# Two products of a feed-forward block moved into the last head of an attention kernel, the last tile mixed on VectorE, the first stores reordered

## The chip, the cores and the metric

One core of one Trainium2 chip runs the kernel. The metric is the device time of one execution in microseconds (us), the median of several runs. A measurement of this kernel can tell a difference of about 0.2% from none.

## The reference

`X` is 2 x 1024 x 128, all fp32. With `xn = layernorm(X)`:

```python
# differential attention, 16 heads, d = 64
A1, A2 = Q1 @ K1.T / 8, Q2 @ K2.T / 8            # each head: 1024 x 1024
Pm = softmax(A1) - lam * softmax(A2)
Y = concat_heads(Pm @ V) @ Wo + bo
attn = layernorm(Y) * gamma + beta, times 0.2
# feed-forward block: one main set and the best 2 of 8 expert sets per batch row
main = gelu(xn @ W1m + b1m) @ W2m + b2m
expert_out = sum_k gate_k * (gelu(xn @ W1e[k] + b1e[k]) @ W2e[k] + b2e[k])
out = X + attn + a * main + (1 - a) * expert_out
```

## The kernel before, in words

Every engine has its own hand-written stream, and semaphores join them. There are three stages.

**Start.** `X` is loaded, normalised by VectorE (DVE) and transposed by TensorE (PE) into `xT_hi` and `xT_lo` (an fp32 value is split into a high and a low part, and a product takes three passes). Query and key of head 0 are projected (`proj`, L540). Then 32 units `values(u)` (L558) make V for all heads; two units are one tile of 128 tokens. Units below 24 run ahead of the attention (L576), the others in its first steps (`V_LATE`). DVE takes three of four units out of PSUM with the bias added (`evac_v`, L992), ScalarE (ACT) the fourth (`copy_v`, L815), and GpSimd (POOL) adds its bias afterwards (`bias_v`, L498). SyncE (SP) stores each tile in HBM (`store_v`, L319); the SBUF buffer `pt` holds eight tiles, so the evacuation of tile i waits until the store of tile i - 8 has landed. On the same SP queue, in program order: `cross_q` (L285, the halves of q exchanged), `load_w` (L300, the weights of a head), `store_w` (L305, their split parts). On POOL, in order: `split_w(1)` (L405), `start_y` (L419), then `bias_v`.

**Attention.** 32 heads (2 batch rows x 16) of 8 query tiles are 256 steps, `STEPS`; `step(g, k)` with a body of 16 steps stands in each engine's stream (L649 PE, L863 ACT, L508 POOL, L1066 DVE). A step n makes the two score matrices of tile n in PSUM (`product`, L590, L597), takes row maxima on DVE (L1044), exponentials on ACT (`exps`, L830, L838), and POOL mixes them one step later (scale L514, add L517). Three steps later PE transposes the mixed tile in two halves (`turn`, L617), ACT evacuates each half (`evac_pt`, L851, L860), and every four tiles PE multiplies by V (`pv`, L633) and, a step later, by Wo (`out_proj`, L645); DVE adds the result to `y_acc` (`add_y`, L1056). Six PSUM banks are three `slot`s, used in turn by the two score tiles of a step and, at steps 2 and 6 of a head, by a projection for the next head (L550), which ACT and DVE take out. The last head (steps 248 to 255) has no projections. Steps 256 to 262 finish the tiles that are still under way. `beside` puts feed-forward work between them: `start_hidden` (L732) issues products 0 to 3, `start_gelu` (L898) GELUs 0 to 2. `high_w1` (L842, ACT) and `low_w1` (L1061, DVE) split the first-layer weights at the steps in `SPLIT_AT`.

**Feed-forward.** 24 units u (2 batch rows x 3 sets x 4 chunks of the hidden layer). `hidden_mm(u)` (L703, six matmuls, L713) writes a slot; `gelu(u)` (L886, L895) takes it to one of four `hidden` buffers in SBUF; `output_mm(u)` (L718, L726) multiplies that by W2 into banks 6 and 7, where the units of a batch row are summed. The waits that carry the stage are these:

```python
# hidden_mm(u): its slot was that of unit u - 3
after(pe, h_done, u - 2)
# gelu(u): its buffer was that of unit u - 4
act.wait_ge(h_mm, u + 1)
after(act, out_mm, u - 3)
# the order on PE, OUT_LAG = 4
for u in range(OUT_LAG, UNITS + OUT_LAG):
    hidden_mm(u)
    output_mm(u - OUT_LAG)
```

`h_done` counts finished GELUs, `out_mm` finished output products. The first output product waits for the last `add_y`. Beside this DVE normalises `y_acc` (`norm_y`, L1104); the square root for it stands on ACT ahead of GELU `SQRT_AT` and needs DVE's variances (`lny`).

Of the kernel before, what the change touches and what calls it, by code (L numbers as in the profile page):

```python
# [33 lines left out]
OUT_LAG = 4  # L34
SPLIT_AT = {STEPS - 1: (0,), STEPS: (1, 2), STEPS + 1: (3, 4)}
V_LATE = {0: (24, 25), 1: (26, 27), 2: (28, 29), 3: (30,), 4: (31,)}
V_EARLY = 24
SQRT_AT = 5
# [10 lines left out]
def build(nc, X, Wq, bq, Wk, bk, Wv, bv, Wo, bo, gamma, beta, lam,  # L49
# [5 lines left out]
    with ExitStack() as ctx:  # L55
# [35 lines left out]
        small = sb("small", 256)  # L91
        top_idx = sb("top_idx", 8, U32)
# [37 lines left out]
        hidden = [pt[:, i * S:(i + 1) * S] for i in range(4)]  # L130
# [32 lines left out]
        w1_high, w1_low, h_mm = sem("w1_high"), sem("w1_low"), sem("h_mm")  # L163
# [36 lines left out]
        def slot_free(g, tile):  # L200

            n = TILES.index(tile) - 3
            g, (k, what) = (g, TILES[n]) if n >= 0 else (g - 1, TILES[n])
            if isinstance(g, int) and (g < 0 or (what == "proj" and not now(g, k, -TB))):
                return None
            if what == "proj":
                return lo_done, 2 * (2 * g + k // TB) + 3 + PROJ_AT.index(k % TB)
            return exp_done, 2 * (g * BODY + k) + what + 1

# [48 lines left out]
        def _(sp):  # L258
# [54 lines left out]

            sp.wait_ge(lo_done, 1)
            cross_q(0)
            load_w(1)
# [11 lines left out]
            for i in range(V_EARLY // 2):  # L328
                store_v(i)
                if i % 2 and i // 2 < NW:  # L330
                    store_w(i // 2)
                    load_w(i // 2 + 2)
# [57 lines left out]
        def _(pool):  # L390
# [101 lines left out]
            pool.tensor_tensor(wv_lo, wv_raw, wv_hi.bitcast(F32), ALU.subtract).then_inc(wv_split, 1)  # L492
            for n in range(1, NW):
                split_w(n)
            pool.wait_ge(xn_ready, 2 * B)
# [12 lines left out]
            def step(g, k):  # L508
                n, km = g * BODY + k, (k - 1) % BODY
                if now(g, k, 1):  # L510
                    e1 = p_mix[:, km % 4 * S:(km % 4 + 1) * S]
                    e2 = e2_buf[:, km % 4 * S:(km % 4 + 1) * S]
                    pool.wait_ge(recip_done, 2 * n)
                    pool.tensor_scalar(e2, e2, l_inv[:, 2 * km + 1:2 * km + 2], l1_neg[:, km % 4:km % 4 + 1],  # L514
                                       ALU.mult, ALU.mult).then_inc(scaled, 1)
                    pool.wait_ge(scaled, n)
                    pool.tensor_tensor(e1, e1, e2, ALU.add).then_inc(mix_done, 1)  # L517
                if k % TB == SPLIT_W_AT and g * 2 + k // TB + NW < H:
                    split_w(g * 2 + k // TB + NW)
                set_main(n)  # L520
                set_expert(n)
# [6 lines left out]
        def _(pe):  # L528
# [72 lines left out]
            def open_turn(g, k, half):  # L601

                n = g * BODY + k - LAG
                if half == 0:
                    if isinstance(g, int) and g * BODY + k == LAG:
                        pe.wait_ge(*v_out(28))
                    pe.wait_ge(mix_done, n + 1)
# [41 lines left out]
            def step(g, k):  # L649
# [18 lines left out]
                if now(g, k):  # L668
# [8 lines left out]
                    product(g, k, 1, 2, 1)  # L677

# [23 lines left out]

            def hidden_mm(u):  # L703
# [3 lines left out]
                after(pe, h_done, u - 2)  # L707
                if c == 0:
                    pe.wait_ge(w1_low, set_ + 1)
                for j, (w, a) in enumerate(((w1_hi, xT_hi), (w1_lo, xT_hi), (w1_hi, xT_lo))):  # L710
                    for half in range(2):
                        t0 = b * S + half * BANK
                        mm = pe.matmul(slot[u % 3][:, half * BANK:(half + 1) * BANK],  # L713
# [4 lines left out]
            def output_mm(u):  # L718
# [5 lines left out]
                for t in range(TB):  # L724
                    out_ps = ps[:, 6 * BANK + t * E:6 * BANK + (t + 1) * E]
                    mm = pe.matmul(out_ps, hidden[u % 4][:, t * P:(t + 1) * P],  # L726
# [5 lines left out]
            def start_hidden(k):  # L732

                if k == 0:
                    pe.wait_ge(exp_done, 2 * STEPS)
                if k < OUT_LAG:
                    hidden_mm(k)
# [4 lines left out]
            switch = UNITS // B + OUT_LAG  # L742
            for u in range(OUT_LAG, UNITS + OUT_LAG):
                if u < UNITS and u != switch + 1:
                    hidden_mm(u)
                if u == switch:
                    hidden_mm(u + 1)
# [8 lines left out]
        def _(act):  # L756
# [93 lines left out]

            def evac_pt(g, k, half):  # L851
# [11 lines left out]
            def step(g, k):  # L863
                p = k - 1
                if p % TB in PROJ_AT and now(g, p, -TB):
                    high_part(g * 2 + p // TB + 1, (p // TB + 1) % 2, PROJ_AT.index(p % TB),
                              slot[SLOT[p, "proj"]])
                if now(g, k, LAG):
                    evac_pt(g, k, 0)
                if now(g, k):  # L870
                    exps(g, k, 0)
                if k % TB in PROJ_AT and now(g, k):
                    exps(g, k, 1)
                if now(g, k, LAG):
                    evac_pt(g, k, 1)
                if k % TB not in PROJ_AT and now(g, k):
                    exps(g, k, 1)
                n, par = g * 2 + k // TB + 1, (k // TB + 1) % 2
                if k % TB == 0 and now(g, k, -TB):
                    next_bias(n, par)  # L880
                if isinstance(g, int) and (g * BODY + k) in SPLIT_AT:
                    for s_ in SPLIT_AT[g * BODY + k]:
                        high_w1(s_)


            def gelu(u):  # L886
# [6 lines left out]
                act.wait_ge(h_mm, u + 1)  # L893
                after(act, out_mm, u - 3)
                act.activation(hidden[u % 4], slot[u % 3], ACT.Gelu_apprx_tanh, bias=b1_col[:, col:col + 1],  # L895
                               scale=1.0).then_inc(h_done, 1)

            def start_gelu(k):  # L898

                if k == 1:  # L900
                    act.wait_ge(set_step, SET_STEPS)
                if 1 <= k <= 3:
                    gelu(k - 1)

            attention(act, step, QB + 3, start_gelu)
            for u in range(3, UNITS):
# [4 lines left out]
        def _(dve):  # L911
# [93 lines left out]
            low_part(0, 0, 0, slot[0])  # L1005
            low_part(0, 0, 1, slot[2])
            low_x(2)
# [5 lines left out]
            dve.wait_ge(rows_loaded, 64)  # L1013
            evac_v(0, 12)
# [45 lines left out]

            def low_w1(s_):  # L1061
# [4 lines left out]
            def step(g, k):  # L1066
# [25 lines left out]
                if j in (0, 2) and not soon and now(g, k, 1):  # L1092
                    inv_sums()
                if isinstance(g, int) and g == 0:
                    for u in V_LATE.get(k, ()):
                        evac_v(u, u + 1)
                if isinstance(g, int) and (g * BODY + k - 1) in SPLIT_AT:
                    for s_ in SPLIT_AT[g * BODY + k - 1]:
                        low_w1(s_)
# [89 lines left out]
```

## Time and profile before

| | |
|---|---|
| median of 3 runs | 1168.79 us (1168.78 to 1169.16) |
| the profiled execution's own time | 1167.64 us |
| its span | 1165.7 us |
| start, to the first scores | about 39 us |
| attention, to the last scores | about 1063 us |
| steps 256 to 262 and the first feed-forward products | about 1063 to 1103 us |
| feed-forward, to the last output product | about 1103 to 1161 us |

Every profile is of one execution. A line of a timeline gives the start and the time of an instruction (or of several merged, x count), and in brackets how long its engine was idle before it and what ended that. The chain of waits is followed back from the last instruction. "Granted clock" is TensorE's, as a share of 2.4 GHz.

### The profile page before, as it was taken

Reading aid. Unit: us, or ns where it says so; the run is one execution under the profiler, and the core shown is the slowest. Engines: PE = TensorE matmul, PEld = TensorE weight load, DVE = VectorE, ACT = ScalarE, POOL = GpSimd, SP = SyncE. Lnnn points to the kernel's source line nnn. Section 1 sums busy time; section 2 is a strip of 40 time slices with the busy share of each in tenths; the row PEclk is TensorE's granted clock in tenths of the full one; section 3 lists DMA queues with packets and bytes.
Section 4 is the critical chain, followed back from the end, with each engine's and each line's share of the span. In section 5 each row is a group of like instructions: output and inputs, shape, how many; then the busy total and the mean of one; then the engine's idle time right before and its main releaser. Section 6 shows DMA issues by size and latency. Waiting matters only on the chain.

```text
span 1165.7 us, 27852 instructions
## 1 busy us (share of the span) xinstructions
PE 1121.7 (96%) x9730; PEld 775.1 (66%) x9730; DVE 903.6 (78%) x1572; ACT 955.4 (82%) x1722; POOL 977.9 (84%) x607
## 2 busy tenths in 40 slices
PE   5899999999999999999999999999999999998898
PEld 4666666666666666666666666666666666665697
DVE  7888888888888888888888888888888888875610
ACT  3598889898889988888988888888889888986432
POOL 2799999999999999999998999999898888996000
PEclk9999999999999999999999999999999999999999
DMA  8733522222221122222212211222222122100000
GB/s 202 290 87 83 126 58 50 62 62 62 62 58 38 45 62 57 56 67 56 56 45 56 53 33 38 57 56 56 56 56 57 45 56 55 28 22 1 1 19 19
DMA packets 76440, 71.28 MB, mean 61 GB/s; under 512 B 43381, under 2 KB 65397, under 8 KB 76405
## 3 DMA queue, kind: packets, MB, share of 16 engines
q1 hardware_dynamic: 75396, 70.65, 23.4%
q8 instruction: 19, 0.31, 0.1%
q10 hardware_dynamic: 880, 0.19, 0.1%
q14 instruction: 17, 0.13, 0.0%
q0 software_dynamic: 128, 0.01, 0.0%
HBM read 22.59 MB, written 14.68 MB: 32 GB/s over the span
## 4 chain that ended last, share of the span: by engine, by line
PE 67%; ACT 22%; issue 6%; DVE 3%; DMA 1%; ACTq 1%; SPq 0%; DVEq 0%
PE ps L633 21%; PE ps L597 19%; ACT work L838 12%; PE ps L617 11%; PE ps L550 9%; ACT p_mix L838 6%; PE ps L726 3%; ACT pt L860 3%; PE ps L713 2%; PE ps L568 1%; PE ps L645 1%; ACT small L792 1%; DMA v_scratch<-pt 0%; DVE pt L1001 0%; DVE p_mix L957 0%
## 5 line engine op out<-in xcount | busy, mean ns | idle before, releaser
L1044 DVE TENSOR_REDUCE small<-ps 128x1 f32<-128x1024 f32 x512 | 613.5, 1219 | 159.2 <-PE ps L597 159.2
L517 POOL TENSOR_TENSOR p_mix<-p_mix,work 128x1024 f32<-128x1024 f32 x256 | 608.9, 2378 | 21.4
L860 ACT ACTIVATE pt<-ps 128x512 f32<-128x512 f32 x512 | 306.9, 599 | 122.4 <-PE ps L617 120.4
L617 PE MATMUL ps<-ident,p_mix 64*128 64x64 f32 x4096 | 351.2, 226 | 4.1 <-issue 2.2
L514 POOL TENSOR_SCALAR work<-work,small 128x1024 f32<-128x1024 f32 x256 | 308.2, 1204 | 43.6 <-DVE small L1074 41.1
L617 PEld LDWEIGHTS ps<-ident,p_mix 64*128 64x128 f32 x4096 | 303.9, 139 | 51.9 <-issue 32.7
L838 ACT ACTIVATE p_mix<-ps,small 128x1024 f32<-128x1024 f32 x256 | 286.5, 1119 | 3.9 <-DVE small L1044 3.9
L838 ACT ACTIVATE work<-ps,small 128x1024 f32<-128x1024 f32 x256 | 285.2, 1114 | 0.2
L633 PE MATMUL ps<-pt,v_h 128*64 128x512 f32 x1024 | 248.1, 605 | 0.7 <-ACT pt L860 0.7
L597 PE MATMUL ps<-k_hi,q_hi 64*128 64x512 f32 x512 | 226.6, 443 | 4.1 <-ACT p_mix L838 3.5
L597 PE MATMUL ps<-k_hi,q_lo 64*128 64x512 f32 x512 | 224.7, 439 | 0.0
L597 PE MATMUL ps<-k_lo,q_hi 64*128 64x512 f32 x512 | 206.6, 403 | 0.0
L597 PE MATMUL ps<-k_hi,qx_hi 64*128 64x512 f32 x512 | 196.5, 460 | 1.3 <-ACT p_mix L838 1.3
L597 PEld LDWEIGHTS ps<-k_hi,q_hi 64*128 64x128 f32 x512 | 94.3, 184 | 137.4 <-ACT p_mix L838 70.6
L597 PE MATMUL ps<-k_lo,qx_hi 64*128 64x512 f32 x512 | 172.6, 397 | 0.0
L597 PE MATMUL ps<-k_hi,qx_lo 64*128 64x512 f32 x512 | 170.4, 392 | 0.0
L633 PEld LDWEIGHTS ps<-pt,v_h 128*64 128x64 f32 x1024 | 62.3, 136 | 94.2 <-issue 93.3
L597 PEld LDWEIGHTS ps<-k_hi,q_lo 64*128 64x128 f32 x512 | 94.4, 184 | 0.0
L597 PEld LDWEIGHTS ps<-k_lo,q_hi 64*128 64x128 f32 x512 | 94.0, 184 | 0.2
L597 PEld LDWEIGHTS ps<-k_lo,qx_hi 64*128 64x128 f32 x512 | 91.6, 185 | 3.0
L597 PEld LDWEIGHTS ps<-k_hi,qx_hi 64*128 64x128 f32 x512 | 81.8, 189 | 17.8 <-ACT work L838 8.1
L597 PEld LDWEIGHTS ps<-k_hi,qx_lo 64*128 64x128 f32 x512 | 92.9, 187 | 0.9
(137 smaller groups left out, 1212.8 us busy)
## 6 DMA issues: line engine op xcount, KB each, us to landing
qx_hi<-q_hi SPq DMA_DIRECT2D x64, 256.0 KB, 3.8
qx_lo<-q_lo SPq DMA_DIRECT2D x64, 256.0 KB, 4.7
v_scratch<-pt SPq DMA_DIRECT2D x16, 512.0 KB, 4.8
v_h<-v_scratch SPq DMA_DIRECT2D x32, 256.0 KB, 3.1
w_scratch<-wqk_hi SPq DMA_DIRECT2D x16, 160.0 KB, 1.8
w_scratch<-wqk_lo SPq DMA_DIRECT2D x16, 160.0 KB, 1.9
wqk_hi<-w_scratch SPq DMA_DIRECT2D x16, 160.0 KB, 2.2
wqk_lo<-w_scratch SPq DMA_DIRECT2D x16, 160.0 KB, 2.3
```

What stands on the lines that cost most here:

```text
L514: pool.tensor_scalar(e2, e2, l_inv[:, 2 * km + 1:2 * km + 2], l1_neg[:, km % 4:km % 4 + 1], ALU.mult, ALU.mult).then_inc(scaled, 1)
L517: pool.tensor_tensor(e1, e1, e2, ALU.add).then_inc(mix_done, 1)
L550: mm = pe.matmul(into[:, half * BANK:(half + 1) * BANK], wt[:, col:col + P], a[:, bass.ds(t0 + half * BANK, BANK)], start=j == 0, stop=j == 2)
L568: mm = pe.matmul(v_bank(u), a[:, i * P:(i + 1) * P], w[:, hv * BANK:(hv + 1) * BANK], start=j == 0, stop=j == 2)
L597: return pe.matmul(slot[SLOT[k, s]][:, half * BANK:(half + 1) * BANK], (ax if half else a)[rows, q0:q0 + P], b[rows, k0 + half * BANK:k0 + ...
L617: mm = pe.transpose(pt_ps[:, c * D:(c + 1) * D], p_mix[rows, col:col + P], ident[rows, rows])
L633: mm = pe.matmul(o_ps[half * D:(half + 1) * D, :], vh4[:, (kb // 2) % 2, c, :], pt4[:, kb % 2, c, :], start=c < 2, stop=c >= KC - 2, skip_ ...
L713: mm = pe.matmul(slot[u % 3][:, half * BANK:(half + 1) * BANK], w[set_][:, c * P:(c + 1) * P], a[:, t0:t0 + BANK], start=j == 0, stop=j == 2)
L726: mm = pe.matmul(out_ps, hidden[u % 4][:, t * P:(t + 1) * P], w24[:, 0 if f == 0 else TOPK * b + f, c, :], start=i == 0 and t % 4 == 0, st ...
L838: act.activation((p_mix, e2_buf)[s][:, k % 4 * S:(k % 4 + 1) * S], slot[SLOT[k, s]], ACT.Exp, bias=neg_max[:, m:m + 1], scale=1.0, accum_o ...
L860: act.activation(pt4[:, kb % 2, :, j * P + half * D:j * P + (half + 1) * D], pt_ps.rearrange("p (c q) -> p c q", c=KC), ACT.Copy).then_inc ...
L1044: dve.tensor_reduce(neg_max[:, m:m + 1], slot[SLOT[k, s]], AX.X, ALU.max, negate=True)\
```

## The change

`OUT_LAG` goes from 4 to 8, `hidden` from 4 buffers to 6 (`HIDDEN`), two of them in a new SBUF tile `h_early`. The products of units 0 and 1 go to steps 250 and 254, the places of the projections that the last head lacks; ACT copies them raw to `h_early` (`keep_hidden`), and their GELUs read them there. Units 2 to 5 are issued in steps 256 to 259 ahead of a transposition, 6 and 7 after steps 260 and 261; GELUs 0 to 5 stand behind ACT's steps 256 to 260. In step 255 ACT takes the second exponential ahead of the evacuation. The last tile is mixed by DVE (`mix_last`), not POOL. `SQRT_AT` goes from 5 to 9. At the start `load_w(1)` is issued ahead of `cross_q(0)`, `store_w` and `load_w` of the next heads behind the first 12 value stores, DVE evacuates values 0 and 1 between the two low parts of head 0 and 2 to 7 ahead of the low parts of `xT`, and POOL's wait for the normalised input stands ahead of `split_w(1)`.

```diff
 W2_AT = (177, 178, 180, 181, 185, 186, 188, 189)
-OUT_LAG = 4
-SPLIT_AT = {STEPS - 1: (0,), STEPS: (1, 2), STEPS + 1: (3, 4)}
+OUT_LAG = 8
+EARLY = {STEPS - 6: 0, STEPS - 2: 1}
+HIDDEN = 6
+GELU_AT = ((0,), (1, 2), (3,), (4,), (5,))
+SPLIT_AT = {STEPS - 8: 0, STEPS: 1, STEPS + 2: 2, STEPS + 3: 3, STEPS + 4: 4}
 V_LATE = {0: (24, 25), 1: (26, 27), 2: (28, 29), 3: (30,), 4: (31,)}
 V_EARLY = 24
-SQRT_AT = 5
+SQRT_AT = 9
 BODY = 2 * TB
...
         small = sb("small", 256)
+        h_early = sb("h_early", 2 * S)
         top_idx = sb("top_idx", 8, U32)
...
                         for t in ((q_hi, qx_hi, k_hi), (q_lo, qx_lo, k_lo)))
-        hidden = [pt[:, i * S:(i + 1) * S] for i in range(4)]
+        hidden = [t[:, i * S:(i + 1) * S] for t, n in ((h_early, 2), (pt, 4)) for i in range(n)]
         y_sq = pt[:, 4 * S:6 * S].rearrange("p (t e) -> p t e", e=E)
...
         pv_done, o_evac, y_mm, y_evac = sem("pv_done"), sem("o_evac"), sem("y_mm"), sem("y_evac")
-        w1_high, w1_low, h_mm = sem("w1_high"), sem("w1_low"), sem("h_mm")
+        w1_high, w1_low, h_mm, h_raw = sem("w1_high"), sem("w1_low"), sem("h_mm"), sem("h_raw")
+        last_step, last_mixed = sem("last_step"), sem("last_mixed")
         h_done, out_mm, f_out = sem("h_done"), sem("out_mm"), sem("f_out")
...
             g, (k, what) = (g, TILES[n]) if n >= 0 else (g - 1, TILES[n])
+            if isinstance(g, int) and what == "proj" and g * BODY + k in EARLY:
+                return h_raw, EARLY[g * BODY + k] + 1
             if isinstance(g, int) and (g < 0 or (what == "proj" and not now(g, k, -TB))):
...
             return exp_done, 2 * (g * BODY + k) + what + 1
+        def h_slot(u):
+            assert SLOT[10, "proj"] == SLOT[14, "proj"] == 0
+            return slot[0] if u < 2 else slot[(u - 1) % 3]
...
         def by_act(u):
...
+            load_w(1)
             sp.wait_ge(lo_done, 1)
             cross_q(0)
-            load_w(1)
...
             def store_v(i):
...
                 store_v(i)
-                if i % 2 and i // 2 < NW:
-                    store_w(i // 2)
-                    load_w(i // 2 + 2)
+            for i in range(NW):
+                store_w(i)
+                load_w(i + 2)
...
             pool.tensor_tensor(wv_lo, wv_raw, wv_hi.bitcast(F32), ALU.subtract).then_inc(wv_split, 1)
+            pool.wait_ge(xn_ready, 2 * B)
             for n in range(1, NW):
                 split_w(n)
-            pool.wait_ge(xn_ready, 2 * B)
             start_y()
...
             def bias_v(first, end):
...
             def step(g, k):
                 n, km = g * BODY + k, (k - 1) % BODY
-                if now(g, k, 1):
+                if now(g, k, 1) and n < STEPS:
                     e1 = p_mix[:, km % 4 * S:(km % 4 + 1) * S]
...
                         pe.wait_ge(*v_out(28))
-                    pe.wait_ge(mix_done, n + 1)
+                    if isinstance(n, int) and n == STEPS - 1:
+                        pe.wait_ge(last_mixed, 1)
+                    else:
+                        pe.wait_ge(mix_done, n + 1)
                 after(pe, pt_evac, 2 * n + half)
...
                     product(g, k, 1, 2, 1)
+                if isinstance(g, int) and 0 <= g * BODY + k - STEPS < 4:
+                    hidden_mm(2 + g * BODY + k - STEPS)
...
+                if isinstance(g, int) and g * BODY + k in EARLY:
+                    pe.wait_ge(*slot_free(g, (k, "proj")))
+                    hidden_mm(EARLY[g * BODY + k])
             def hidden_mm(u):
...
                 set_ = 0 if f == 0 else TOPK * b + f
-                after(pe, h_done, u - 2)
+                if u == 2:
+                    pe.wait_ge(exp_done, 2 * STEPS - 1)
+                if u == 3:
+                    pe.wait_ge(exp_done, 2 * STEPS)
+                if u == 4:
+                    pe.wait_ge(h_raw, 2)
+                if u > 4:
+                    pe.wait_ge(h_done, u - 2)
                 if c == 0:
...
                         t0 = b * S + half * BANK
-                        mm = pe.matmul(slot[u % 3][:, half * BANK:(half + 1) * BANK],
+                        mm = pe.matmul(h_slot(u)[:, half * BANK:(half + 1) * BANK],
                                        w[set_][:, c * P:(c + 1) * P],
...
                     out_ps = ps[:, 6 * BANK + t * E:6 * BANK + (t + 1) * E]
-                    mm = pe.matmul(out_ps, hidden[u % 4][:, t * P:(t + 1) * P],
+                    mm = pe.matmul(out_ps, hidden[u % HIDDEN][:, t * P:(t + 1) * P],
                                    w24[:, 0 if f == 0 else TOPK * b + f, c, :],
...
             def start_hidden(k):
...
-                if k == 0:
-                    pe.wait_ge(exp_done, 2 * STEPS)
-                if k < OUT_LAG:
-                    hidden_mm(k)
+                if k in (4, 5):
+                    hidden_mm(k + 2)
...
-            switch = UNITS // B + OUT_LAG
             for u in range(OUT_LAG, UNITS + OUT_LAG):
-                if u < UNITS and u != switch + 1:
+                if u < UNITS:
                     hidden_mm(u)
-                if u == switch:
-                    hidden_mm(u + 1)
                 if u == OUT_LAG:
...
+            def keep_hidden(u):
+                act.wait_ge(h_mm, u + 1)
+                act.activation(h_early[:, u * S:(u + 1) * S], h_slot(u), ACT.Copy).then_inc(h_raw, 1)
             def evac_pt(g, k, half):
...
                               slot[SLOT[p, "proj"]])
+                last = isinstance(g, int) and g * BODY + k == STEPS - 1
+                if isinstance(g, int) and g * BODY + p in EARLY and not last:
+                    keep_hidden(EARLY[g * BODY + p])
                 if now(g, k, LAG):
...
                     exps(g, k, 0)
-                if k % TB in PROJ_AT and now(g, k):
+                if (k % TB in PROJ_AT or last) and now(g, k):
                     exps(g, k, 1)
...
                     evac_pt(g, k, 1)
-                if k % TB not in PROJ_AT and now(g, k):
+                if k % TB not in PROJ_AT and not last and now(g, k):
                     exps(g, k, 1)
+                if last:
+                    keep_hidden(EARLY[g * BODY + p])
                 n, par = g * 2 + k // TB + 1, (k // TB + 1) % 2
...
                 if isinstance(g, int) and (g * BODY + k) in SPLIT_AT:
-                    for s_ in SPLIT_AT[g * BODY + k]:
-                        high_w1(s_)
+                    high_w1(SPLIT_AT[g * BODY + k])
...
             def gelu(u):
...
                 col = (0 if f == 0 else TOPK * b + f) * HC + c
-                act.wait_ge(h_mm, u + 1)
-                after(act, out_mm, u - 3)
-                act.activation(hidden[u % 4], slot[u % 3], ACT.Gelu_apprx_tanh, bias=b1_col[:, col:col + 1],
+                if u < 2:
+                    act.wait_ge(h_raw, u + 1)
+                else:
+                    act.wait_ge(h_mm, u + 1)
+                if u == 2:
+                    act.wait_ge(pv_done, STEPS // QB - 1)
+                after(act, out_mm, u - HIDDEN + 1)
+                act.activation(hidden[u % HIDDEN], h_early[:, u * S:(u + 1) * S] if u < 2 else h_slot(u), ACT.Gelu_apprx_tanh, bias=b1_col[:, col:col + 1],
                                scale=1.0).then_inc(h_done, 1)
...
             def start_gelu(k):
...
-                if k == 1:
+                if k == 0:
                     act.wait_ge(set_step, SET_STEPS)
-                if 1 <= k <= 3:
-                    gelu(k - 1)
+                for u in GELU_AT[k] if k < len(GELU_AT) else ():
+                    gelu(u)
...
             attention(act, step, QB + 3, start_gelu)
-            for u in range(3, UNITS):
+            for u in range(HIDDEN, UNITS):
                 gelu(u)
...
             low_part(0, 0, 0, slot[0])
+            dve.wait_ge(rows_loaded, 64)
+            evac_v(0, 2)
             low_part(0, 0, 1, slot[2])
+            evac_v(2, 8)
             low_x(2)
...
             dve.tensor_scalar(mean_tok, mean_tok, 1.0 / S, None, ALU.mult).then_inc(route, 1)
-            dve.wait_ge(rows_loaded, 64)
-            evac_v(0, 12)
+            evac_v(8, 12)
             dve.wait_ge(route_mm, 1)
...
+            def mix_last():
+                c = (STEPS - 1) % BODY
+                factor, e1, e2 = small[:, 246:247], p_mix[:, c % 4 * S:(c % 4 + 1) * S], e2_buf[:, c % 4 * S:(c % 4 + 1) * S]
+                dve.wait_ge(recip_done, 2 * STEPS)
+                dve.tensor_tensor(factor, l_inv[:, 2 * c + 1:2 * c + 2], l1_neg[:, c % 4:c % 4 + 1], ALU.mult)\
+                    .then_inc(last_step, 1)
+                dve.wait_ge(last_step, 1)
+                dve.scalar_tensor_tensor(out=e1, in0=e2, scalar=factor, in1=e1, op0=ALU.mult, op1=ALU.add)\
+                    .then_inc(last_mixed, 1)
             def low_w1(s_):
...
                     inv_sums()
+                if isinstance(g, int) and g * BODY + k == STEPS:
+                    mix_last()
                 if isinstance(g, int) and g == 0:
...
                 if isinstance(g, int) and (g * BODY + k - 1) in SPLIT_AT:
-                    for s_ in SPLIT_AT[g * BODY + k - 1]:
-                        low_w1(s_)
+                    low_w1(SPLIT_AT[g * BODY + k - 1])
                 if j == 0 and now(g, k - j, 2 * QB):
...
```

## Rows read from the trace of the kernel before

**Rows 1.** The page of the profile: engines' busy time, and one of its costliest groups.

```profile
PE 1121.7 (96%) x9730; PEld 775.1 (66%) x9730; DVE 903.6 (78%) x1572; ACT 955.4 (82%) x1722; POOL 977.9 (84%) x607
...
L860 ACT ACTIVATE pt<-ps 128x512 f32<-128x512 f32 x512 | 306.9, 599 | 122.4 <-PE ps L617 120.4
```

**Rows 2.** The chain that ended last, from 1040 us on: start us, us, what.

```profile
1085.87 1.89 PE ps L633 x8
...
1088.53 1.17 PE ps L645 x8
...
1089.72 1.14 DVE y_acc L1056 x4
...
1100.39 0.18 DVE small L1129
...
1106.73 1.38 PE ps L713 x6
...
1152.34 8.95 PE ps L726 x80
```

**Rows 3.** Stretches: busy time of PE, PEld, DVE, ACT, POOL, granted clock, DMA share, GB/s.

```profile
1061.00:1062.00 1.00, 1.00 (x7) 0.89 (x6) 0.14 (x2) 0.31 (x1) 0.92 (x2) 0.50 0.00 0
1079.00:1083.00 4.00, 1.59 (x14) 0.91 (x14) 0.75 (x3) 3.13 (x5) 0.00 (x0) 1.00 0.01 4
1104.00:1161.00 57.00, 57.00 (x415) 53.13 (x413) 6.43 (x7) 19.12 (x18) 0.00 (x0) 1.00 0.03 10
```

**Rows 4.** The timeline of all engines, feed-forward stage: start us, us, engine, line, names.

```profile
1104.79 1.95 PE L726 MATMUL ps<-w,pt 128*128 128x128 f32 x16
...
1106.49 0.71 PE L713 MATMUL ps<-xT_hi,qx_hi 128*128 128x512 f32 x2
...
1106.83 1.12 ACT L895 ACTIVATE pt<-ps,b_col 128x1024 f32<-128x1024 f32 x1 [1.57 <-PE ps L726]
```

**Rows 5.** The timeline of DVE, the start.

```profile
19.17 1.27 DVE L981 SCALAR_TENSOR_TENSOR q_lo<-ps,small,q_hi 128x1024 fp32r<-128x1024 f32 x1
...
36.53 0.69 DVE L1001 TENSOR_TENSOR pt<-ps,o_t 128x512 f32<-128x512 f32 x1 [1.75 <-DMA v_scratch<-pt]
...
40.31 1.93 DVE L1001 TENSOR_TENSOR pt<-ps,o_t 128x512 f32<-128x512 f32 x3 [0.74 <-DMA v_scratch<-pt]
42.16 2.34 DVE L1044 TENSOR_REDUCE small<-ps 128x1 f32<-128x1024 f32 x2
44.92 1.29 DVE L1001 TENSOR_TENSOR pt<-ps,o_t 128x512 f32<-128x512 f32 x2 [0.42 <-DMA v_scratch<-pt]
```

**Rows 6.** The timelines of PE, SP and POOL, the start.

```profile
23.90 0.49 PE L568 MATMUL ps<-k_hi,xT_hi 128*128 128x512 f32 x1 [1.73 <-DVE pt L1001]
...
37.37 0.85 SPq L326 DMA_DIRECT2D v_scratch<-pt  x2
...
27.74 0.45 POOL L409 TENSOR_SCALAR wqk_raw<-wqk_raw,small 128x128 f32<-128x128 f32 x1 [11.77 <-DMA wqk_raw<-in_L_attn_Wq]
```

**Rows 7.** The timeline of PE: a projection and a step's scores, in two heads.

```profile
962.53 0.73 PE L550 MATMUL ps<-xT_hi,wqk_hi 128*128 x2 [0.16 <-ACT work L838]
...
996.02 0.50 PE L597 MATMUL ps<-k_hi,q_hi 64*128 64x512 f32 x1
...
1026.34 0.74 PE L550 MATMUL ps<-xT_hi,wqk_hi 128*128 128x512 f32 x2 [0.16 <-ACT work L838]
...
1059.77 0.50 PE L597 MATMUL ps<-k_hi,q_hi 64*128 64x512 f32 x1 [1.73 <-ACT p_mix L838]
```

**Rows 8.** The timeline of ACT, the last steps.

```profile
1066.70 1.11 ACT L838 ACTIVATE work<-ps,small 128x1024 f32<-128x1024 f32 x1
...
1077.92 1.28 ACT L895 ACT_TABLE_LOAD   x1
1079.22 1.11 ACT L895 ACTIVATE pt<-ps,b_col 128x1024 f32<-128x1024 f32 x1
```

**Rows 9.** The timeline of POOL, the last tile's mix.

```profile
1070.13 2.37 POOL L517 TENSOR_TENSOR p_mix<-p_mix,work 128x1024 f32<-128x1024 f32 x1
```

## The prediction

> **What bounds the kernel now.** I read the page's busy times first: PE is busy 96% of the span, no other engine over 84% [rows 1]. Such a share hides stages with different limits, so I then followed the chain of waits from its end. From 1106 us on it is PE alone: a first-layer product takes 1.38 us, and the last five output products take 8.95 us, 1.79 each, ending at 1161.3 [rows 2]. The stretch from 1104 to 1161 shows PE busy for all of its 57 us at the full granted clock (2.4 GHz) [rows 3]. So before the change this stage has no hole: a unit costs 1.38 + 1.79 = 3.17 us, and ACT, 19 us busy in 57, has room. What lets PE run through is seen in its timeline [rows 4]: output product 4 starts at 1104.79 and ends at 1106.74; the GELU that this frees starts at 1106.83; PE does not wait for it and has started the next first-layer product at 1106.49. Two more outputs lie between that GELU and the product that needs it.
>
> The first output product waits for the last addition to `y_acc`, which ends at 1089.72 + 1.14 = 1090.9 [rows 2]. Five first-layer products stand ahead of it.
>
> At the start the limit is another. DVE waits for the landing of value stores 1.75, 0.74 and 0.42 us, and the first row maximum comes at 42.16 [rows 5]. PE waits 1.73 us for an evacuation, SP issues the third store only at 37.37, and POOL waits until 27.74 for the weights of head 1 with its bias additions queued behind [rows 6].
>
> **The change, part by part.** *Start.* `load_w(1)` no longer stands behind a wait for DVE and four issues; POOL splits the weights some 4 us earlier, and its bias additions, on which the second store waits, follow. The ten issues of `store_w` and `load_w` leave the place ahead of the stores; behind the twelfth they take as long as before, and `load_v` and stores 12 to 14, queued behind them, are still issued a little earlier than now, as their readers are. DVE evacuates values 0 and 1 ahead of the key's low part, which takes PE's wait of 1.73 away; the low parts of `xT` then come late, but only value 16 needs them. I take the four waits, 1.73 + 1.75 + 0.74 + 0.42 = 4.64, as gained: **-4.7**. From below it is 2.5 (only the two longer waits of DVE, if stores that come closer together queue up), from above 6 (PE's small waits as well). The attention is a chain of buffers, so all its steps move by this.
>
> *Last head.* Product 0 and 1 take the place, slot and length of a projection, and the raw copy on ACT (1024 columns, 1.1) that of the projection's high part. What a head with its projections costs is in the trace: from a projection to the scores 10 steps later 33.49 us; where the later projection is missing, 33.43, because PE then waits 1.73 for ACT instead [rows 7]. So the two products are hidden, **+0.1**. The cover is ACT's and POOL's pace; without it they would cost 2.8.
>
> *Steps 255 to 262.* After that idle time PE's granted clock is 0.50 at 1061 us [rows 3], the 1.2 GHz level, and the last scores are slow. With product 1 in the gap I expect the full clock, about 1.2 us. The second exponential ended at 1067.8 [rows 8] behind an evacuation that waited for PE; now it follows the first and ends at 1065.2. DVE's mix is a tiny product and one pass over 1024 columns, priced by the 1.27 of the like pass [rows 5], and ends at 1067.4, where POOL's ended at 1072.5 [rows 9]. POOL's mix of tile 254 reads SBUF at the same time; both together may stretch it by the 1.27, and its reader comes 3 us later, so nothing. But this gain isn't the stage's: ACT is late next. Its stream now runs, with 0.5 to 0.6 for an evacuation [rows 1]: second half of tile 252 1065.8, raw copy 1066.9, 253 first half 1067.5; PE then does 1.9 of V; 253 second half 1070.1, split 1070.6, table load and GELU 0 (1.28 + 1.11 [rows 8]) 1073.0; only then the evacuation of 254, on which PE waits about 1 us, 1074.9; GELUs 1 and 2 1077.1; tile 255 1079.0, another 1.3 of PE's time lost. PE goes on with product 5 to 1079.8, four pieces of V (1.9 for two) to 1083.6, product 6 to 1085.0, Wo 1.1, products 7 and 8 to **1088.9** [rows 2]. There the first output starts, 2.0 us earlier than before, and with nine products done and not five.
>
> One rule bears on this. The trace has the table load of 1.28 us with the GELU 0.02 behind it [rows 8]. The Trainium skill (ScalarE: Activation LUTs, What ACT_TABLE_LOAD costs) puts a drain of about 1.38 us on top, 2.66 for a switch; by it alone, with the evacuation of 254 queued behind GELU 0, the sum would be 1.4 us higher. I go by the trace.
>
> *Feed-forward.* Remaining: 24 outputs x 1.79 and 15 products x 1.38 = 63.7 us, which would end at 1152.6, 8.7 earlier than now. But the order and the buffers no longer fit. Product u + 3 needs the slot of unit u, so GELU u; GELU u needs the buffer of unit u - 6, so output u - 6 (`out_mm` at u - 5); and on PE, with a lag of 8, output u - 6 stands directly ahead of product u + 3. Three slots and six buffers hold nine units, and nine are under way. So PE stands still for each GELU from 6 to 20, ahead of products 9 to 23: fifteen times. The price of one stands in [rows 4]: the next product could start at 1106.49, the freed GELU runs from 1106.83 for 1.12, and PE takes some 0.05 to follow: 1108.0, so 1.5 us. 15 x 1.5 = **+22.6** (from 1.25 to 1.6 each: 19 to 24). The last eight outputs have no product between them and don't wait. The end comes at 1175.2 in place of 1161.3: +13.9.
>
> `SQRT_AT` at 9 costs nothing: the variances are ready 9.7 us after the last addition (1100.6 against 1090.9 [rows 2]), GELU 9 waits for output 3, 17 us after it, and two table loads and the square root fit ahead of it. The dropped exchange at unit 16 costs nothing: while DVE takes out the first batch row, PE waits for GELU 17 and makes product 20.
>
> **Sum.** -4.7 + 0.1 + 13.9 = +9.3 on the profiled execution's 1167.6: 1176.9. The median of the runs lies 1.15 above that execution, so 1178.0.
>
> **The rivals.** *Faster: the stalls do not decide.* If a GELU did not have to wait for the output just ahead (the point from which this decides is a stall below 0.3 us each), the same sum gives -4.7 + 0.1 - 8.7: 1155.5. For it: the lag of 4 shows no wait at all. Against it: the indices, and a GELU that is released by an output in every period [rows 4]. 6 in 100. *Slower still: the clock falls.* PE would idle in every period, and once it fell behind 1.73 us of idle [rows 3, 7]. Against it: around 1079 to 1083 PE was busy for only 1.59 of 4 us at clock 1.00 [rows 3], and 1.5 in 4.7 is less idle than that. If half of the periods ran at 1.2 GHz, their 3.17 would double: +24, 1202. 6 in 100. The Trainium skill (TensorE: Matmul & The Clock Gate, Part 1) says that the throttled state is the default and activity releases it; by that, sparser work has the risk, but both rows are needed to size it. *The start gives nothing* (the stores queue in the DMA engines, or SP is late with `load_v`): 1182.7. 8 in 100.
>
> **How the numbers follow.** The forecast has 80 in 100. Its bounds: start 2.5 to 6, the tail's start 2 us either way, the stalls 19 to 24, together 1171 to 1184; with the third case the range 1171 to 1185 holds 88, which leaves room for what I have overlooked. Slower by over 0.2% (2.3 us, about what a measurement of this kernel tells from none): all but the first rival and a little of the low edge, 0.92. Same 0.02, faster 0.06.
>
> **What would show it.** In the feed-forward stage: PE busy about 70%, its product line with 15 waits of 1.2 to 1.5 us for the GELU, each GELU released by an output, a unit every 4.7 us. First output at about 1084 (1088.9 less the start). At the start: first row maximum near 37.5, no waits of DVE for stores. Last scores at clock 1.00. It is wrong if the stage shows PE without waits, or if its clock shows 0.5 there.

## The result and the profile after

| | median | runs | ratio to before |
|---|---|---|---|
| before | 1168.97 us | 4 (1168.78 to 1169.40) | |
| after | 1182.31 us | 4 (1181.80 to 1182.97) | 1.0116, 95% interval 1.0102 to 1.0129 |

The changed kernel is 13.3 us slower. Its profiled execution took 1182.97 us, with a span of 1181.2. In its code the lines have other numbers: a first-layer product is L742 (L713 before), an output product L755 (L726), a GELU L933 (L895), a transposition L633 (L617), a score product L610 (L597), a row maximum L1084 (L1044).

The page's busy times say little, as before: PE still counts as busy for 95% of the span. This line answers to [rows 1].

```profile
PE 1127.4 (95%) x9730; PEld 776.9 (66%) x9730; DVE 908.0 (77%) x1574; ACT 957.8 (81%) x1724; POOL 975.9 (83%) x605
```

The chain that ended last shows it. Its columns are those of [rows 2].

```profile
1087.19 1.80 PE ps L755 x16
...
1089.07 1.12 ACT h_early L933
...
1090.24 1.66 PE ps L742 x6
1091.90 1.80 PE ps L755 x16
...
1103.17 1.28 ACT L933
1104.46 1.12 ACT pt L933
1105.59 0.04 issue
1105.63 2.00 PE ps L742 x6
1107.63 3.07 PE ps L755 x16
...
1160.65 16.09 PE ps L755 x144
```

Before, the chain was PE alone from 1106 us on. Now an output (1087.19) is followed by the GELU that it frees (1089.07) and only then by the next product (1090.24): PE, ACT, PE, in every unit. The last nine outputs run without a gap, 16.09 us, and end at 1176.7; before they ended at 1161.3 [rows 2].

PE's timeline after gives the holes, in brackets, and what ended them.

```profile
21.64 0.63 PE L581 MATMUL ps<-k_lo,xT_hi 128*128 128x512 f32 x1
...
1056.43 0.73 PE L742 MATMUL ps<-xT_hi,q_hi 128*128 128x512 f32 x2 [0.17 <-ACT work L862]
...
1072.14 0.68 PE L633 MATMUL ps<-ident,p_mix 64*128 64x64 f32 x8 [0.93 <-ACT pt L889]
...
1076.13 0.68 PE L633 MATMUL ps<-ident,p_mix 64*128 64x64 f32 x8 [1.08 <-ACT pt L889]
...
1090.24 0.73 PE L742 MATMUL ps<-xT_hi,qx_hi 128*128 128x512 f32 x2 [1.26 <-ACT h_early L933]
...
1105.63 0.73 PE L742 MATMUL ps<-xT_hi,q_hi 128*128 128x512 f32 x2 [2.54 <-ACT pt L933]
```

There are fifteen holes from product 9 to 23, fourteen of 1.26 us and one of 2.54; each unit takes 4.70 us (3.17 before). Stretches of the trace after, in the columns of [rows 3]:

```profile
1061.00:1062.00 1.00, 1.00 (x8) 0.29 (x4) 1.00 (x1) 1.00 (x2) 1.00 (x2) 1.00 0.00 0
1088.00:1159.00 71.00, 50.76 (x317) 44.11 (x317) 16.65 (x20) 19.49 (x18) 0.00 (x0) 0.98 0.03 8
1108.00:1110.00 2.00, 2.00 (x12) 2.00 (x11) 1.57 (x2) 0.00 (x0) 0.00 (x0) 0.50 0.00 0
```

The last scores run at the full clock where they had 0.50 before. In the stage PE is busy for 71% of the time (50.76 of 71 us). Behind the long hole, at 1108 us, the granted clock is 0.50, the 1.2 GHz level: the product there takes 2.00 us and not 1.66, the output 3.07 and not 1.80.

The account of the two profiled executions: the scores of step 255 come 1.75 us earlier (1059.77 [rows 7] to 1058.02), the first output 3.9 earlier (1090.9 to 1087.03), the last output ends 15.4 later.

### The profile page after: what moved, and what is told of

Its sections match the earlier page's. It is cut to its first block, busy times and chain, and to the rows that moved or that the text cites. A ratio compares the mean times of both kernels' runs of the same rounds, so it can differ in the third digit from the quotient of the medians.

```text
span 1181.2 us, 27853 instructions
## 1 busy us (share of the span) xinstructions
PE 1127.4 (95%) x9730; PEld 776.9 (66%) x9730; DVE 908.0 (77%) x1574; ACT 957.8 (81%) x1724; POOL 975.9 (83%) x605
## 4 chain that ended last, share of the span: by engine, by line
PE 67%; ACT 24%; issue 6%; DVE 2%; ACTq 1%; DMA 0%; DVEq 0%; SPq 0%
PE ps L649 21%; PE ps L610 19%; ACT work L862 12%; PE ps L633 10%; PE ps L563 9%; ACT p_mix L862 6%; PE ps L755 4%; ACT pt L889 3%; PE ps L742 3%; PE ps L581 1%; ACT pt L933 1%; ACT h_early L933 1%; ACT small L816 0%; DMA x_all<-in_L_attn_X 0%; ACTq L816 0%
## 5 line engine op out<-in xcount | busy, mean ns | idle before, releaser
L1084 DVE TENSOR_REDUCE small<-ps 128x1 f32<-128x1024 f32 x512 | 613.5, 1219 | 157.6 <-PE ps L610 157.6
L530 POOL TENSOR_TENSOR p_mix<-p_mix,work 128x1024 f32<-128x1024 f32 x255 | 607.5, 2382 | 21.3
L633 PE MATMUL ps<-ident,p_mix 64*128 64x64 f32 x4096 | 350.6, 226 | 2.2 <-ACT pt L889 2.0
L633 PEld LDWEIGHTS ps<-ident,p_mix 64*128 64x128 f32 x4096 | 303.2, 138 | 50.8 <-issue 31.3
L610 PE MATMUL ps<-k_hi,q_hi 64*128 64x512 f32 x512 | 226.5, 442 | 0.6 <-DVE q_lo L1019 0.6
L610 PE MATMUL ps<-k_hi,q_lo 64*128 64x512 f32 x512 | 224.6, 439 | 0.0
L610 PE MATMUL ps<-k_lo,q_hi 64*128 64x512 f32 x512 | 206.4, 403 | 0.0
L610 PE MATMUL ps<-k_hi,qx_hi 64*128 64x512 f32 x512 | 196.5, 459 | 0.0
L610 PEld LDWEIGHTS ps<-k_hi,q_hi 64*128 64x128 f32 x512 | 94.1, 184 | 134.3 <-ACT p_mix L862 60.2
L610 PE MATMUL ps<-k_lo,qx_hi 64*128 64x512 f32 x512 | 173.1, 397 | 0.0
L610 PE MATMUL ps<-k_hi,qx_lo 64*128 64x512 f32 x512 | 170.4, 391 | 0.0
L610 PEld LDWEIGHTS ps<-k_hi,q_lo 64*128 64x128 f32 x512 | 94.2, 184 | 0.0
L610 PEld LDWEIGHTS ps<-k_lo,q_hi 64*128 64x128 f32 x512 | 93.9, 183 | 0.2
L610 PEld LDWEIGHTS ps<-k_lo,qx_hi 64*128 64x128 f32 x512 | 91.3, 184 | 3.2
L610 PEld LDWEIGHTS ps<-k_hi,qx_lo 64*128 64x128 f32 x512 | 92.6, 187 | 1.0
L610 PEld LDWEIGHTS ps<-k_hi,qx_hi 64*128 64x128 f32 x512 | 81.6, 189 | 16.9 <-ACT work L862 8.5
```

Source lines behind the costliest of these rows:

```text
L610: return pe.matmul(slot[SLOT[k, s]][:, half * BANK:(half + 1) * BANK], (ax if half else a)[rows, q0:q0 + P], b[rows, k0 + half * BANK:k0 + ...
L633: mm = pe.transpose(pt_ps[:, c * D:(c + 1) * D], p_mix[rows, col:col + P], ident[rows, rows])
L1084: dve.tensor_reduce(neg_max[:, m:m + 1], slot[SLOT[k, s]], AX.X, ALU.max, negate=True)\
```

## The experiments

**1. A lag of 7.** One output more ahead of product 9; buffers, slots and all else unchanged.

```diff
-            for u in range(OUT_LAG, UNITS + OUT_LAG):
+            for u in range(OUT_LAG, UNITS + 7):
...
-                if u >= OUT_LAG:
-                    output_mm(u - OUT_LAG)
+                for v in (0, 1) if u == OUT_LAG else (u - 7,):
+                    output_mm(v)
```

> The changed kernel with one thing altered: two output products follow product 8, so the lag on PE is 7 instead of 8 (same buffers, same slots). Theory A (nine units fill three slots and six buffers, so each GELU from 6 to 20 stands between an output and the next product): with a lag of 7 one more output lies between the GELU and the product that needs it, 1.79 us against the 1.2 to 1.5 of the wait, so all 15 waits vanish (15 x 1.54 = 23.1 us) and with them the longer hole around the square root and the slow clock behind it (1.3 + 1.6): about 1156.5 us, ratio to the kernel before near 0.989. Rival B (the stage is slow because PE's clock or the table switch suffers, not the order): at most 3 us come back, 1179. Rival C (the new buffers or the reads from h_early are slow): nothing changes, 1182.

Measured: 1156.87 us, 0.9903 (0.9889 to 0.9917) of the kernel before: 25.4 us less than the changed kernel, from one unit of lag. Its stretch from the first output to 1150 us, its only hole there, and the table load behind the square root:

```profile
1086.00:1150.00 64.00, 63.84 (x474) 59.64 (x473) 18.22 (x22) 22.88 (x21) 0.00 (x0) 1.00 0.03 9
```

```profile
1123.49 2.02 PE L755 MATMUL ps<-w,h_early 128*128 128x128 f32 x16 [0.16 <-DVE y_acc L1205]
```

```profile
1096.74 1.28 ACT L933 ACT_TABLE_LOAD   x1 [0.50 <-PE ps L755]
```

PE is busy for 63.84 of 64 us. The table load still stands behind its GELU's wait, but now PE has an output to do meanwhile. The hole of 0.16 is output 12 waiting for DVE, where the exchange at unit 16 was dropped.

**2. Eight buffers, lag of 8.** The order on PE is that of the changed kernel. Two buffers are added, and with them ACT waits once, ahead of GELU 6, for the last multiplication by V, whose part of `pt` they take.

```diff
-HIDDEN = 6
+HIDDEN = 8
...
-        hidden = [t[:, i * S:(i + 1) * S] for t, n in ((h_early, 2), (pt, 4)) for i in range(n)]
+        hidden = [t[:, i * S:(i + 1) * S] for t, ns in ((h_early, (0, 1)), (pt, (0, 1, 2, 3, 6, 7))) for i in ns]
...
-            for u in range(HIDDEN, UNITS):
+            act.wait_ge(pv_done, STEPS // QB)
+            for u in range(6, UNITS):
```

> The changed kernel with 8 hidden buffers instead of 6 (the two new ones in the part of pt that the last multiplication by V frees), lag 8 and the order on PE unchanged. Theory A: three slots and eight buffers hold eleven units for nine under way, no wait, about 1156.5 us as with lag 7. Rival D (the lag of 8 itself is bad, whatever the buffers, because products run too far ahead): 1182 as now. B as for lag 7: 1179.

Measured: 1156.57 us, 0.9897 (0.9883 to 0.9912), the same as a lag of 7. So neither the lag nor the buffers are at fault alone: the stall comes from a lag that is exactly slots + buffers - 1.

**3. The kernel before with a lag of 6.** `OUT_LAG = 6`, four buffers, the exchange at unit 16 taken out.

> The kernel before with OUT_LAG 6 in place of 4 (4 buffers, and without the exchange at unit 16). Theory A, as a rule (a lag of slots + buffers - 1 has no slack): three slots and four buffers hold seven units and seven are under way, so products 7 to 23 each wait for a GELU; 15 waits of 1.5 us and two outputs that no longer run while the square root is awaited (3.6 us): 1190 to 1198 us, about 1195. Rival (more lag costs nothing or helps, the waits in the changed kernel come from something else in it): 1167 to 1172 us.

Measured: 1197.70 us, 1.0252 (1.0237 to 1.0267), at the top of A's range. PE's timeline has the same holes, seventeen of them ahead of products 7 to 23 where the expectation counts 15: sixteen of 1.26 us, and a longer one where the square root is awaited:

```profile
1096.60 0.72 PE L713 MATMUL ps<-xT_hi,q_hi 128*128 128x512 f32 x2 [1.26 <-ACT pt L892]
...
1104.43 1.22 PE L713 MATMUL ps<-xT_hi,qx_hi 128*128 128x512 f32 x2 [4.39 <-ACT pt L892]
...
1111.24 0.74 PE L713 MATMUL ps<-xT_hi,qx_hi 128*128 128x512 f32 x2 [1.26 <-ACT pt L892]
```

```profile
1104.00:1108.00 4.00, 3.57 (x10) 3.00 (x11) 3.86 (x5) 0.37 (x1) 0.00 (x0) 0.50 0.02 4
```

The stall needs nothing of the early products, the new tile or the start. The clock fell inside the hole of 4.39 us (1.00 until 1102 us, 0.58 in the next) and is 0.50 behind it, which the 1195 expected did not contain.

**4. The table loaded early.** The changed kernel, with a GELU of one column behind the square root.

```diff
                     act.activation(std_x, var_x, ACT.Sqrt).then_inc(lny_sqrt, 1)
+                    act.activation(small[:, 248:249], one, ACT.Gelu_apprx_tanh)
```

> The changed kernel (lag 8) with a GELU of one column directly behind the square root, so that the GELU table is loaded before ACT waits for output 3. Theory E (the hole ahead of product 12 is 2.54 us and not 1.26 because the table load stands behind the wait, and PE's clock falls to 1.2 GHz behind a hole of that length): hole 1.26, clock 1.00 through the stage, 1.3 + 1.6 = 2.9 us less, 1179.4 us. Rival F (the clock falls from the general sparseness of the stage, somewhere, hole or not): 1181.0. Rival G (the load costs PE nothing): 1182.3.

Measured: 1179.66 us, 1.0094 (1.0074 to 1.0114). Its product 12 and the clock of its stage:

```profile
1103.25 0.73 PE L742 MATMUL ps<-xT_hi,q_hi 128*128 128x512 f32 x2 [1.26 <-ACT pt L934]
```

```profile
1085.00:1157.00 72.00, 53.04 (x340) 46.08 (x339) 18.54 (x22) 19.70 (x19) 0.00 (x0) 1.00 0.03 8
```

Theory E holds: the hole is 1.26, the clock stays at 1.00 although PE is busy for only 74%, and 2.7 us are gone.

**5. The square root at GELU 12.** `SQRT_AT = 12` in the changed kernel.

> The changed kernel (lag 8) with the square root ahead of GELU 12 instead of 9. Theory E (the hole of 2.54 us comes from the table load that waits with its GELU, and the clock falls behind it): the hole of 2.54 us moves from product 12 to product 15, the granted clock is 1.00 where it fell before and falls, if at all, only behind the new hole; time 1179.4 to 1182.3 us. Rival F (the clock falls wherever the stage is sparse): it falls at another place than behind the hole.

Measured: 1184.23 us (two runs).

```profile
1105.50 0.73 PE L742 MATMUL ps<-xT_hi,q_hi 128*128 128x512 f32 x2 [1.26 <-ACT pt L933]
...
1120.89 0.73 PE L742 MATMUL ps<-xT_hi,q_hi 128*128 128x512 f32 x2 [2.54 <-ACT h_early L933]
```

```profile
1076.00:1080.00 4.00, 4.00 (x16) 2.05 (x16) 1.39 (x2) 3.60 (x6) 0.00 (x0) 0.64 0.02 4
1122.00:1124.00 2.00, 2.00 (x9) 1.71 (x8) 1.93 (x3) 0.00 (x0) 0.00 (x0) 0.50 0.03 8
```

The hole of 2.54 us moved to product 15, and the slow clock with it. The time lies above what either theory said. In the profiled execution the clock also fell at about 1077 us, behind the two waits of steps 258 and 259 (0.93 and 1.08, as in the changed kernel's timeline), and from the second of them to product 9 it took 15.7 us where the changed kernel took 14.1, so 1.6 us. There the changed kernel's clock had held. So the place of the fall behind a hole is shown, twice; that it falls behind every such hole is not.

**6. The start, whole and in its two parts,** each alone in the kernel before (the diff's hunks for the start; for 6b those of SP and POOL, for 6c those of DVE).

6a: 

> The kernel before with only the start of the change (load_w(1) ahead of cross_q(0), store_w and load_w behind the twelve stores, the new order of evacuations on DVE, POOL's wait ahead of split_w). What the trace of the changed kernel says: the steps run 1.75 us earlier than before, so 1167.2 us, -0.15%. What was forecast: 4.7 us earlier, 1164.3 us, -0.4%, if the half clock of PE around 21 to 24.6 us in the changed kernel's profile was chance. A third reading: nothing at all, 1169.

6b: 

> The kernel before with the reordered queues of SP and POOL alone (DVE's evacuations in the old order). The sum of the forecast gave it DVE's three waits for stores, 2.9 us: 1165.7. Theory S (waits of one chain overlap and the tiny routing operations on DVE stretch while POOL runs): it is most of the start's 3.1 us, 2 to 2.9 us less, 1165.7 to 1166.6 us. Rival: nothing alone, 1168.6.

6c: 

> The kernel before with the new order of evacuations on DVE alone. The sum of the forecast gave it PE's wait of 1.73 us: 1166.9. Theory S: PE is earlier but the stores still land late, so the same row maximum comes at the same time, 0 to 0.5 us less, 1168.1 to 1168.6 us.

| | median | ratio (95%) |
|---|---|---|
| 6a, whole | 1165.55 (11 runs) | 0.9975 (0.9967 to 0.9984) |
| 6b, SP and POOL | 1167.52 (12 runs) | 0.9993 (0.9982 to 1.0004) |
| 6c, DVE | 1168.91 (11 runs) | 1.0000 (0.9992 to 1.0009) |

The whole start is worth 3.1 us, between the two readings of 6a. 6b misses its range (about 1.5 us, not clear of nothing), 6c gives nothing. The two parts together give 1.5 of the 3.1, a difference only just beyond the intervals. Their profiles show what the time went into. First 6b's PE, then 6c's DVE:

```profile
24.90 0.50 PE L568 MATMUL ps<-k_hi,xT_hi 128*128 128x512 f32 x1 [2.26 <-DVE pt L1001]
```

```profile
36.05 0.69 DVE L1001 TENSOR_TENSOR pt<-ps,o_t 128x512 f32<-128x512 f32 x1 [2.95 <-DMA v_scratch<-pt]
```

With DVE's order alone, PE's wait is gone and DVE's first wait for a store has grown from 1.75 [rows 5] to 2.95. With the queues alone, PE's wait is 2.26. This profile is not a clean witness, though: behind that wait the granted clock is 0.57 from 26 to 30 us, and the first row maximum comes at 42.37 us, no earlier than before. The reading that fits all three is that the waits stand behind one another on one path, so that each part takes away little without the other. In 6a's DVE and PE both are gone, and something else has come:

```profile
27.12 1.21 DVE L1015 TENSOR_SCALAR small<-small 128x2 f32<-128x2 f32 x1
...
35.82 1.27 DVE L1031 TENSOR_TENSOR small<-small 2x1 f32<-2x1 f32 x1
```

```profile
28.98 0.50 PE L568 MATMUL ps<-k_hi,xT_hi 128*128 128x512 f32 x1 [1.22 <-DVE pt L1001]
```

Two operations on one or two columns take 1.2 us each, and an evacuation behind the first comes late for PE. (The kernel before has one such operation too, 1.19 us at 37.32, with a wait for a store behind it.) In 6c, which has the same order on DVE, the first of the two and the one ahead of it are short. Here they are, and behind them POOL's additions in 6a:

```profile
26.65 0.15 DVE L1013 TENSOR_TENSOR small<-small 128x2 f32<-128x2 f32 x1
26.84 0.17 DVE L1015 TENSOR_SCALAR small<-small 128x2 f32<-128x2 f32 x1
```

```profile
25.76 2.54 POOL L503 TENSOR_TENSOR pt<-pt,o_t 128x512 f32<-128x512 f32 x2
```

In 6c POOL does nothing until 27.95 us. In 6a it is adding: its second addition ends at 28.30, and DVE's operation that began at 27.12 ends at 28.33.

**7. The start undone in the best version.** Lag of 7, start as before.

> The changed kernel with a lag of 7 and the start as in the kernel before. Theory: the start is worth what it was worth alone, about 3.1 us, so 1156.9 + 3.1 = 1160.0 us, ratio to before about 0.9925, and the tail with its earlier products is the rest, 8.7 to 9 us. Rival (the start was worth the forecast 4.7 and the start-only run lost some of it to the clock in the last head): 1161.6. Rival (start nearly worthless here): 1157.

Measured: 1159.77 us, 0.9922 (0.9907 to 0.9937): the start is worth 2.9 there (against the 1156.87 of experiment 1 and the 1156.86 of experiment 8), and the tail with its earlier products 8.7.

**8. POOL mixes the last tile.** Lag of 7, `mix_last` taken out.

> The changed kernel with a lag of 7 and the last tile mixed by POOL as before. Theory H (ACT's queue, not the mix, sets steps 256 to 258: the mix would end at about 1069 and its first reader comes at 1074.3): nothing, 1156.9 us within 0.5. Rival (the DVE mix is what shortened the tail, 5 us earlier): 1159 to 1161.

Measured: 1156.86 us, 0.9897 (0.9880 to 0.9914), the same as experiment 1. PE's two waits in steps 258 and 259 are unchanged:

```profile
1071.07 0.69 PE L630 MATMUL ps<-ident,p_mix 64*128 64x64 f32 x8 [0.93 <-ACT pt L886]
...
1075.06 0.68 PE L630 MATMUL ps<-ident,p_mix 64*128 64x64 f32 x8 [1.08 <-ACT pt L886]
```

**9. The GELU table in ACT's idle time.** Lag of 7, a GELU of one column behind the first evacuation of step 256.

> The changed kernel with a lag of 7 and a GELU of one column behind the first evacuation of step 256, where ACT is idle for 1.91 us: the table load of 1.28 leaves the stretch in which the evacuations of tile 254 wait for ACT. Theory H: PE's waits of 0.93 and 1.08 us in steps 258 and 259 shrink to near 0 and near 1, 1 to 1.3 us less, 1155.7 us. Rival (a later wait of the same queue takes it back, since GELUs 1 and 2 stand ahead of tile 255): 1156.9. If it is the fastest, it is the version to keep.

Measured: 1156.84 us, 0.9896 (0.9878 to 0.9913), no change in the median. In its trace the wait of 0.93 is gone and this one is left:

```profile
1073.86 0.68 PE L633 MATMUL ps<-ident,p_mix 64*128 64x64 f32 x8 [1.08 <-ACT pt L889]
```

From product 1 to the first output it takes 29.7 us, the version with a lag of 7 alone 30.6. So 0.9 us is seen locally, and five runs that scatter over 2.4 us don't show it in the whole.

The versions with a lag of 7 or with eight buffers beat both kernels, by 1.0% against the kernel before.

## Why the prediction was right, and which terms were off

*The verdict and its cause.* Slower was right, and so was the reason: a stall ahead of products 9 to 23, each for a GELU that waits for the output just ahead. The forecast priced one at 1.5 us; the unit takes 4.70 us against 3.17, so 1.53, and fifteen make 23.0 against the 22.6 on record. Experiments 1 to 3 show the cause from three sides: one unit of lag less or two buffers more take all of it away, and the kernel before gets it with a lag of 6 and nothing else of the change but the dropped exchange. The time is inside the range and 4.3 us above the forecast, because the start gave less and two costs were priced at nothing. The faster rival's sum without stalls was 1155.5; with a lag of 7 the time is 1156.9.

*Last head, steps 255 to 262.* Products 0 and 1 are hidden: from the first row maximum to the scores of step 255 it takes 1017.6 us before and 1017.9 after, so 0.3 and not 0.1. The full clock at 1061 us came as said. The length of the tail was right to 0.1: from the scores of step 255 to the first output the forecast had 29.0 us (1059.9 to 1088.9), the trace has 29.0 (1058.02 to 1087.03), with ACT's queue as its limit and PE's two waits at 0.93 and 1.08 us, forecast at about 1 and 1.3. That the last tile's mix is worth nothing holds (experiment 8). The table load costs 1.28 us with its GELU directly behind it, also at 1103.17; the Trainium skill's drain on top (ScalarE: Activation LUTs, What ACT_TABLE_LOAD costs) is not seen here.

*The start, mis-sized.* The term "1.73 + 1.75 + 0.74 + 0.42 = 4.64, as gained" took four waits of one path as if each stood alone. It measures 3.1 us (experiment 6). All four are gone in the trace after, and DVE waits for no store; yet the first row maximum comes at 40.15 us, not near 37.5. In the profiled execution the steps ran only 1.75 earlier. A part of that is PE's clock, which was at half from about 21.3 to 24.6 us (a value matmul of 0.63 us in PE's timeline, 0.39 elsewhere). The other seven profiles with this start have the full clock there, and their first row maximum comes at 38.95 to 39.86 us.

*The square root, wrong.* "`SQRT_AT` at 9 costs nothing ... two table loads and the square root fit ahead of it." The first load and the root do. The second stands behind its GELU's wait for the output (1103.17, released by PE), so it lengthens that hole by 1.28 us. In the trace before, the same load ran straight behind the root (at 1100.83), because the output that its GELU needs had ended long before; with a lag of 8 that output is the last thing to come.

*The clock.* The rival priced a fall in half of the periods. What came is one fall in the stage, behind the longest hole, for 0.34 + 1.27 = 1.6 us, which the sum had at nothing. Experiment 4 takes away the longer hole and with it the fall: 2.7 us. One of the signs of being wrong was that the clock shows 0.5 in the stage. Taken by the letter, the row of 1108 us is that sign; over the whole stage the clock is 0.98, and the holes cost 24.3 us against its 1.6.

The sum: the forecast had +9.3, measured are +13.3. In the profiled execution the last output ends at 1176.7, the forecast's sum puts it at 1170.6; of the 6.1 between, 2.9 are the start, 1.3 the table load, 1.6 the clock and 0.3 the stalls. Between the medians, where the start is worth 3.1, the same terms make 4.8 for the 4.3 measured.

## What to carry to other kernels

Count what is in flight before a lag is raised: where slots + buffers hold N units, a lag of N - 1 runs without deadlock and stalls at every unit (N = 9 and N = 7 here), while N - 2 leaves one instruction of the other kind to cover the stage in between (N = 9; its 1.79 us were longer than the stall of 1.53). A wait on one engine that is released by the operation directly ahead of the reader is the sign of it. Waits in one chain don't add up: take the gain of several from the next thing that the path would wait for. And look where a table load stands: GELU's came behind its wait for the output (1103.17), while in the kernel before the one for the root ran at 1094.19 and the root itself only at 1100.60, when DVE released it. A tiny activation ahead of the wait moved GELU's.

## What was unexpected of the hardware

*PE's clock.* It fell to the 1.2 GHz level behind both holes of 2.54 us (the changed kernel and experiment 5), inside the one of 4.39 and behind a wait of 2.26 (6b). Shorter waits had it both ways. The five profiled kernels without products 0 and 1 in the last head (before, 3, 6a, 6b, 6c) each have two waits of 1.73 to 1.75 us there, and the clock fell in or behind eight of the ten; in the eight profiles with the products in those places the waits are gone, and no fall is seen there. A wait of 1.73 at the start of the kernel before (at 23.90) brought none. The waits of 0.93 and 1.08 did in experiment 5 and in no other profile that has them. And in the changed kernel the clock fell at about 21.3 us with no wait longer than 0.60 close ahead. Fifteen holes of 1.26 us in a row did not bring it down: the granted clock of such a stage, busy for 74%, was 1.00 (experiment 4).

*DVE held by POOL.* The factor of `mix_last`, one column, took 1.56 us. DVE's and POOL's timelines of the changed kernel:

```profile
1063.80 1.56 DVE L1107 TENSOR_TENSOR small<-small 128x1 f32<-128x1 f32 x1
1065.39 1.28 DVE L1110 SCALAR_TENSOR_TENSOR p_mix<-work,small,p_mix 128x1024 f32<-128x1024 f32 x1
```

```profile
1062.96 2.38 POOL L530 TENSOR_TENSOR p_mix<-p_mix,work 128x1024 f32<-128x1024 f32 x1
```

It ends at 1065.36, POOL's addition at 1065.34. The forecast had POOL's operation stretched; in fact DVE's ended with POOL's. Not every small operation is held: the reciprocal and the scaling just ahead of it, at 1063.49 and 1063.57, took 0.17 and 0.20 us beside the same addition. The Trainium skill (SBUF — State Buffer, Terms) says that the two engines share a pair of ports which one holds for its whole instruction while the other is blocked; the trace agrees in the two ends. Experiment 6 has the comparison: two operations of 0.15 and 0.17 us with POOL idle (6c) take 0.45 and 1.21 beside POOL's additions (6a), and 6a's other one, at 35.82, ends at 37.09 with POOL's at 37.08. So small operations that end with POOL's are held by it, as far as two runs can show it that differ in SP's queue too. The factor itself was never run without POOL beside it, and that the ports are the reason is the page's; no run here can tell.
